# A two-layer transformer kernel: one-off setup work behind the first projections, three small jobs moved between engines, and later arrival times in the planner that writes the order

## The chip, the cores and the metric

One Trainium2 chip; the kernel runs on one of its cores. The metric is the device time of one execution in microseconds (us), median of several runs. Engines are named as in the profile: PE is TensorE (matmuls; PEld its weight loads), DVE is VectorE, ACT is ScalarE, POOL is GpSimd, SP is SyncE, which issues the DMAs.

## The reference

Two pre-norm transformer layers on x of shape (8, 1024, 256), 16 heads of 16 dimensions, all float32:

```
x = x + attention0(layernorm(x))      # causal softmax attention, 16 heads
x = x + ffn0(layernorm(x))            # gates from entmax over 16 experts
x = x + attention1(layernorm(x))      # low-rank q, k, v (folded to 256x256), rotary on half of each head
x = x + ffn1(layernorm(x))            # shared expert relu(x W1)^2 W2, and a router that adds nothing below a gate of 1
```

The part of `ffn0` that the change touches is entmax: 16 logits per token are normalised, sorted in descending order, and for every k the mean and the mean of squares of the k largest are needed, which are running sums over k divided by k:

```
mean   = cumsum(zs) / k
meansq = cumsum(zs * zs) / k
delta  = (1 - k * (meansq - mean**2)) / k
tau    = mean - sqrt(max(delta, 0))
```

The part of `attention1` is the rotary embedding, `x * cos + rot(x) * sin`.

## The kernel before, in words

**Tiles.** The 1024 tokens of a batch are two halves `c` of 512. Everything that is computed per half: a normalisation (`rstd` on POOL, `norm` on ACT, then `xt`, the transposed half, by PE and ACT), the q and k projection (`qk_`, `qk`) and the values (`v_`, `v`), the output projection (`yt`, `ao`), and the feed-forward pieces (`lg`, `logit`, `ent` 1 to 6, `at`, `g`, `h1`, `hid`, `z`, `fo` for layer 0; `rt`, `route`, `up`, `gate`, `down` for layer 1).

**Attention** works on units `u` of one batch, layer, half of the queries and four heads: 128 units. Float32 accuracy comes from three bfloat16 parts stacked along the contraction. A unit goes through these steps:
- `s`: scores with queries on partitions (L1092), read by DVE for the row maximum, one tile of up to 512 columns after another (`maximum`, L1688 on the tile with the causal diagonal, L1691 elsewhere).
- `mx`, `mt`: POOL splits the maxima in three parts, PE transposes them (L1105), DVE copies the 12 x 512 result to `mT` (`max_rows`, L1702), and SP writes it by DMA into the stacked queries `stk_q` (L947).
- `st`: the same scores transposed, maximum subtracted (L1116); ACT takes the exponential (L1428), POOL zeroes the part above the diagonal (L1595).
- `pv`: PE multiplies with the values (L1134); ACT copies (`o`), PE transposes back, DVE divides (`nm`).

PSUM: bank 5 collects `pv`; the other seven are handed out to whatever PE writes next, and PE waits until the last reader of a bank is done.

**q and k** are split for the stack by a chain over ACT and POOL (`rest`, `p1`, `p2`), for layer 1 behind the rotary embedding: POOL multiplies with cos (`rot`, L1571), DVE swaps neighbours (L1676) and multiplies with sin (L1678, `swap_pairs`), POOL adds (`add`, L1602), ACT rounds (`p0`). SP stores the parts in DRAM and loads each unit's stack from there (`ld`).

**Setup.** `fold` transposes and multiplies the low-rank weights of layer 1 into 256 x 256 ones and turns three feed-forward weights (PE L1253 to L1275, results copied by ACT L1463 and DVE L1864 in turn). It needs fifteen DMAs of weights, and DVE's memsets must be over.

**The order.** Nothing is scheduled by the chip: `program_order()` walks through a model of the engines while the kernel is built, and each engine executes its own instructions in the order of that one list, waiting on semaphores for the others. The model has a table `TIMES` (PE time, then engine and length of what follows), five chains of steps, seven banks, and a rank for each kind of step that could start now; `at` marks in a step's `("after", item)` what it must follow. `windows()` says which chains of steps run beside which attention passes: chain 0 must be finished in its window, chain 1 may go on longer. A step's start in the plan is the time when its inputs are ready by the model. If they come later on the chip, PE stands at that step, and everything behind it stands too.

In `program_order` the setup came as soon as the first window opened, as a fixed 18 us:

```
        if setup:
            plan.put(("setup",), plan.pe)
            plan.pe += 18.0
```

and `windows()` began with

```
    out = [([], [], loaded(0, 0) + loaded(0, 1) + projection(0, 0, 0)), ([(0, 0, 0)], [], projection(0, 0, 1))]
```

## Time and profile before

| | us |
|---|---|
| median of 3 runs | 3171.22 |
| lowest and highest run | 3166.03, 3175.09 |
| the profiled execution, its own time | 3174.84 |
| its span, first to last instruction | 3173.1 |
| busy: PE | 2888.2 (91%) |
| busy: DVE | 2165.5 (68%) |
| busy: ACT | 1905.3 (60%) |
| busy: POOL | 1138.1 (36%) |
| mean granted TensorE clock | 0.950 of 2.4 GHz |

The page of the profile has the busy time of each engine, the span in 40 slices with the granted clock, the chain of work that ended last, and the costliest groups of instructions. The trace behind it answers for any stretch: who waited for whom, the instructions in order of time, and busy times of chosen windows. In a row of the chain of waits or of groups, what stands behind `<-` is what the engine waited for.

### The profile page before, as it was taken

The page shows a single profiled execution, that of the slowest core. Times are in us where ns is not written, and L with a number is a line of the kernel's source. Part 1 is how long each engine was busy: PE and PEld are TensorE (multiplying, and loading weights), DVE is VectorE, ACT ScalarE, POOL GpSimd, SP SyncE. Part 2 cuts the span into 40 slices and gives each one's busy share as a digit, 9 for nine tenths or more (in the row PEclk, how much of TensorE's full clock was granted, in tenths as well). Part 3 has the DMA queues.
Part 4 walks back from the last instruction along what each step waited for, and adds up shares of the span by engine and source line. Part 5 has one row for each costly group of instructions (what it writes and reads, how often), then busy time and mean ns, then how long its engine had stood idle before and what let it go on. Part 6 is the DMA issues. An engine that isn't in the chain of part 4 may idle for free.

```text
span 3173.1 us, 55225 instructions
## 1 busy us (share of the span) xinstructions
PE 2888.2 (91%) x17687; PEld 1366.4 (43%) x17687; DVE 2165.5 (68%) x5957; ACT 1905.3 (60%) x3740; POOL 1138.1 (36%) x2476
## 2 busy tenths in 40 slices
PE   5787999999899998999989998999989999899996
PEld 3433443445344453445534454344534445344432
DVE  4573687765878558775577766776677865878582
ACT  3455655766466664767547674675746766466654
POOL 2314441435324342244513355132541435324421
PEclk9888999999899998999989999999989999899998
DMA  5602442323424253333514245132442324423230
GB/s 153 157 19 64 94 101 50 82 74 99 103 60 106 58 132 73 67 82 93 132 38 89 59 118 126 36 84 56 116 119 54 87 71 116 96 59 83 67 86 22
DMA packets 241196, 268.25 MB, mean 85 GB/s; under 512 B 19568, under 2 KB 208912, under 8 KB 240912
## 3 DMA queue, kind: packets, MB, share of 16 engines
q1 hardware_dynamic: 240912, 264.66, 35.5%
q8 instruction: 154, 2.52, 0.3%
q14 instruction: 130, 1.06, 0.1%
HBM read 162.35 MB, written 100.66 MB: 83 GB/s over the span
## 4 chain that ended last, share of the span: by engine, by line
PE 63%; DVE 18%; ACT 10%; issue 3%; DMA 3%; SPq 2%; POOL 1%; ACTq 0%; POOLq 0%; DVEq 0%
PE ps L1134 14%; PE ps L1116 13%; PE ps L1092 10%; PE ps L1072 6%; DVE mx L1691 6%; PE ps L1064 5%; ACT probs L1428 5%; DVE ps L1688 4%; PE ps L1210 4%; PE ps L1205 3%; PE ps L1197 2%; PE ps L1052 2%; DMA stk_k<-k 1%; ACT xn L1377 1%; PE ps L1097 1%
## 5 line engine op out<-in xcount | busy, mean ns | idle before, releaser
L1428 ACT ACTIVATE probs<-ps 128x512 f32<-128x512 f32 (+1 forms) x2432 | 1228.9, 595 | 429.0 <-PE ps L1116 421.6
L1691 DVE TENSOR_REDUCE mx<-ps 128x1 f32<-128x512 f32 (+2 forms) x1408 | 893.8, 683 | 238.8 <-PE ps L1092 132.6
L1092 PE MATMUL ps<-stk_k,stk_q 112*128 112x512 bf16 (+3 forms) x3072 | 809.9, 339 | 94.2 <-DVE mx L1691 31.2
L1595 POOL TENSOR_SCALAR_AFFINE_SELECT probs<-probs 128x128 f32<-128x128 f32 (+2 forms) x1408 | 479.9, 349 | 866.0 <-ACT probs L1428 836.5
L1116 PE MATMUL ps<-stk_q,stk_k 115*128 115x512 bf16 (+3 forms) x3072 | 758.3, 332 | 27.5 <-DMA stk_q<-mT 21.0
L1688 DVE CUSTOM_DVE_ANT_0 ps<-ps,mask_b 128x512 f32<-128x512 f32 (+1 forms) x1024 | 613.3, 649 | 137.7 <-PE ps L1092 133.2
L1134 PE MATMUL ps<-probs,vaug 128*17 128x512 f32 (+3 forms) x6144 | 586.9, 494 | 11.2 <-ACT probs L1428 6.7
L1092 PEld LDWEIGHTS ps<-stk_k,stk_q 112*128 112x128 bf16 x3072 | 276.4, 98 | 510.1 <-issue 363.5
L1116 PEld LDWEIGHTS ps<-stk_q,stk_k 115*128 115x128 bf16 x3072 | 269.0, 98 | 451.3 <-issue 206.2
L1064 PE MATMUL ps<-turned,wqkv 128*128 128x512 f32 x512 | 269.6, 615 | 9.9 <-ACT turned L1364 5.8
L1134 PEld LDWEIGHTS ps<-probs,vaug 128*17 128x17 f32 x6144 | 138.2, 97 | 313.3 <-issue 188.4
L1614 POOL CAST mparts<-mx 128x16 bf16<-128x16 f32 x128 | 26.4, 206 | 523.4 <-DVE mx L1696 309.3
L1377 ACT ACTIVATE xn<-x,shift,rstd 128x256 f32<-128x256 f32 x256 | 139.2, 618 | 90.8 <-POOL shift L1560 90.8
L1713 DVE RECIPROCAL rec<-ps 128x16 f32<-128x16 f32 x128 | 31.8, 248 | 219.2 <-PE ps L1142 218.7
L1580 POOL TENSOR_TENSOR scratch<-scratch,parts 128x512 f32<-128x512 f32 x128 | 148.2, 1158 | 81.1 <-ACT scratch L1395 43.3
L1449 ACT ACTIVATE scratch<-ps 128x512 f32<-128x512 f32 x128 | 75.5, 597 | 163.9 <-PE ps L1205 163.7
L1364 ACT ACTIVATE turned<-ps 128x512 f32<-128x512 f32 x192 | 114.3, 610 | 89.2 <-PE ps L1052 52.7
L1585 POOL TENSOR_TENSOR parts<-scratch,parts 128x512 bf16<-128x512 f32 x128 | 147.7, 1161 | 35.0 <-ACT parts L1407 34.9
L1721 DVE TENSOR_TENSOR x<-ps,x 128x512 f32<-128x512 f32 x128 | 88.1, 688 | 103.5 <-PE ps L1072 103.5
L1435 ACT ACTIVATE oT<-ps 128x512 f32<-128x512 f32 x128 | 77.9, 609 | 134.1 <-PE ps L1134 132.1
L1571 POOL TENSOR_TENSOR scratch<-scratch,cos 128x512 f32<-128x512 f32 x64 | 81.8, 1279 | 191.7 <-ACT scratch L1395 191.7
L1688 DVE DVE_READ_ACCUMULATOR2_ANT mx<- 128x1 f32 x1024 | 143.2, 140 | 0.0
(155 smaller groups left out, 3128.3 us busy)
## 6 DMA issues: line engine op xcount, KB each, us to landing
k<-parts SPq DMA_DIRECT2D x128, 384.0 KB, 3.5
stk_q<-q SPq DMA_DIRECT2D x256, 192.0 KB, 4.1
stk_k<-k SPq DMA_DIRECT2D x128, 384.0 KB, 6.7
q<-parts SPq DMA_DIRECT2D x64, 384.0 KB, 3.0
stk_k<-k SPq DMA_DIRECT2D x128, 192.0 KB, 4.2
x<-in_L_attn_x SPq DMA_DIRECT2D x16, 512.0 KB, 4.9
k<-parts SPq DMA_DIRECT2D x64, 128.0 KB, 3.5
stk_q<-q SPq DMA_DIRECT2D x128, 64.0 KB, 6.2
```

Source lines behind the costliest of these rows:

```text
L1064: ins = pe.matmul(pt, wqkv[l][:, kd, D * w + P * m:D * w + P * (m + 1)], xT(2 * l, b, c, kd), start=kd == 0, stop=kd == KD - 1)
L1072: ins = pe.matmul(pt[:, D * i:D * (i + 1)], left(kd)[:, cols], right(kd), start=kd == 0, stop=kd == n_k - 1)
L1092: ins = pe.matmul(out[:, width * a:width * (a + 1)], q, stk_k[0:ROWS_S, slot, h + a, BANK * p:BANK * p + width], start=a == 0, stop=a == n ...
L1116: ins = pe.matmul(out[:, width * k:width * (k + 1)], stk_k[0:ROWS, slot, h + k, P * j:P * (j + 1)], stk_q[0:ROWS, slot, h + k, cols], star ...
L1134: ins = pe.matmul(o_bank[32 * h:32 * h + DH + 1, cols], vaug[:, v, j % TPC, HG * g + h, :], probs[:, STEP[u, j] % PBUF, h, cols], start=j ...
L1377: ins = act.activation(xn[:, t, :], src[:, t, :], ACT.Identity, bias=shift[:, i, t:t + 1], scale=rstd[:, i, t:t + 1])
L1428: act.activation(probs[:, step % PBUF, h:h + k, cols], src, ACT.Exp, scale=SCALE)\
L1580: pool.tensor_tensor(q, q, parts[:, o % PRING, 0], ALU.subtract).then_inc(rest_ready, 1)
L1585: pool.tensor_tensor(parts[:, o % PRING, 2], qf[o % QRING], parts[:, o % PRING, 1], ALU.subtract)\
L1595: pool.affine_select(out=diag, in_=diag, compare_op=ALU.is_ge, fill=0.0, base=0, pattern=[[0, k]] * (k > 1) + [[1, P]], channel_multiplier ...
L1688: dve.tensor_tensor_reduce(tile, tile, mask_b[:, BANK - width:BANK], 1.0, LOWEST, ALU.add, ALU.max, most)\
L1691: dve.tensor_reduce(most, tile.rearrange("q (k w) -> q k w", k=k), AX.X, ALU.max)\
```

## The change

Seven things.
1. The setup becomes a step at the end of the first chain, behind the first projection, and the projection of the second half is put in chain 0 beside it. Transposed scores may not start before it. The normalisation and projection of the second batch's first half start one window earlier.
2. The running sums of entmax, eight instructions on DVE (two copies and two additions in part 3, two and two in part 4), become one `tensor_tensor_scan` over all 8 groups of 16: state = going * state + value, where `going` is 0 at each group's first element and 1 elsewhere. Two memsets fill `going` once.
3. The copy of the transposed maxima to `mT` goes from DVE to ACT.
4. The product with sin goes from DVE to POOL, into `rotate`, ahead of its addition. The swap stays on DVE.
5. The router's weights share a tile with entmax's projection; both narrow products now use all 24 columns, and the reader takes other columns. One memset goes.
6. Plan: `TIMES` of `rot` and `add` follow item 4; `max_rows` is planned on ACT with 0.6 us.
7. Plan: `LATER` adds 1.5 us to the time when a step that begins with `xt` may start, 0.7 us for `yt` and `at`; `ROWS_LATER` adds 1.5 us to the arrival of a unit's maxima in `stk_q`.

The `max_rows` in the diff stands in ACT's program; the one on DVE goes.

```diff
+SETUP_TIME, SETUP_LOADED = 20.0, 20.0
-    "rot": (0.0, ("DVE", 1.5), ("POOL", 1.0)), "add": (0.0, ("POOL", 1.2)), "p0": (0.0, ("ACT", 0.63)),
+    "rot": (0.0, ("DVE", 0.75), ("POOL", 1.25)), "add": (0.0, ("POOL", 2.6)), "p0": (0.0, ("ACT", 0.63)),
+LATER = {"xt": 1.5, "yt": 0.7, "at": 0.7}
+ROWS_LATER = 1.5
...
-    out = [([], [], loaded(0, 0) + loaded(0, 1) + projection(0, 0, 0)), ([(0, 0, 0)], [], projection(0, 0, 1))]
+    out = [([], projection(0, 0, 1), loaded(0, 0) + loaded(0, 1) + projection(0, 0, 0) + [([("setup",)], "")]),
+           ([(0, 0, 0)], [], loaded(1, 0) + projection(1, 0, 0))]
...
-            out.append(([(0, 0, 1)], attended(0, 0, 0) + first_ffn(0, 0), ahead + first))
+            out.append(([(0, 0, 1)], attended(0, 0, 0) + first_ffn(0, 0), first))
...
+        if step[0] and step[0][0][0] == "setup":
+            return max(time, SETUP_LOADED)
+        time += later(step)
...
-        end = self.on("DVE", self.pe + HOP, 0.4)
+        end = self.on("ACT", self.pe + HOP, 0.6)
...
-        self.rows[u] = self.transfer(end, 1.4, 0.1)
+        self.rows[u] = self.transfer(end, 1.4, 0.1) + ROWS_LATER
...
-        if u not in self.rows:
+        if u not in self.rows or ("setup",) not in self.at:
...
+            def max_rows(u):
+                pt = arrived(act, ("mt", u))
+                if MT["mt", u]:
+                    act.wait_ge(m_loaded, 16 * MT["mt", u])
+                act.activation(mT[:], pt[0:NP * HG, 0:BANK // 2].bitcast(BF16), ACT.Copy).then_inc(read_out(("mt", u)), 1)
...
             def rotate(*key):
+                pool.wait_ge(swap_ready, r + 1)
+                pool.tensor_tensor(qs[w], qs[w], sin[:, BANK * key[2]:BANK * (key[2] + 1)], ALU.mult).then_inc(sin_ready, 1)
                 pool.wait_ge(cos_ready, r + 1)
...
-                    a = cum[:, 0]
-                    for r, s in enumerate((1, 2)):
-                        z = cum[:, 1 + r % 2]
-                        dve.tensor_copy(z[:, :, 0:s], a[:, :, 0:s])
-                        link(dve.tensor_tensor(z[:, :, s:E0], a[:, :, s:E0], a[:, :, 0:E0 - s], ALU.add))
-                        a = z
+                    flat = [v.rearrange("p t k -> p (t k)") for v in (going[:], cum[:, 0], cum[:, 2])]
+                    link(dve.tensor_tensor_scan(flat[2], flat[0], flat[1], 0.0, ALU.mult, ALU.add))
```

Since the plan is walked anew, the order of all engines changes from the first instruction to the last. Three places show how.

**PE, the start of the program.** `ident,xn` is a half's `xt`, `turned,wqkv` and `wqkv,turned` its projections, `ident,probs` to `ident,scratch` the setup, `stk_k,stk_q` scores. Before:

```order
L1253 MATMUL ps<-ident,probs 128x128 x16
L1259 MATMUL ps<-probs,scratch 32x256 x8
L1266 MATMUL ps<-ident,x 128x128 x4
L1271 MATMUL ps<-ident,scratch 128x128 x8
L1275 MATMUL ps<-ident,scratch 128x128 x2
L1052 MATMUL ps<-ident,xn 128x128 x8
L1064 MATMUL ps<-turned,wqkv 128x512 x8
L1072 MATMUL ps<-wqkv,turned 128x256 x8
L1052 MATMUL ps<-ident,xn 128x128 x8
L1064 MATMUL ps<-turned,wqkv 128x512 x7
L1092 MATMUL ps<-stk_k,stk_q 128x512 x4
```

(of the first three rows each stands three times in turn.) With the change:

```order
L1058 MATMUL ps<-ident,xn 128x128 x8
L1070 MATMUL ps<-turned,wqkv 128x512 x8
L1078 MATMUL ps<-wqkv,turned 128x256 x8
L1058 MATMUL ps<-ident,xn 128x128 x8
L1070 MATMUL ps<-turned,wqkv 128x512 x8
L1078 MATMUL ps<-wqkv,turned 128x256 x8
L1259 MATMUL ps<-ident,probs 128x128 x16
```

Both halves are projected ahead of the setup, the second half first; the scores follow the setup.

**PE, behind the logits of batch 3, first half** (`ident,narrow`). `mparts` is `mt`, `stk_q,stk_k` is `st`, `probs,vaug` is `pv`. Before:

```order
L1177 MATMUL ps<-ident,narrow 128x128
L1092 MATMUL ps<-stk_k,stk_q 128x512 x2
L1092 MATMUL ps<-stk_k,stk_q 128x256 x2
L1097 MATMUL ps<-mask_b,ident_b 128x2x128
L1092 MATMUL ps<-stk_k,stk_q 128x256 x2
L1097 MATMUL ps<-mask_b,ident_b 128x2x128
L1092 MATMUL ps<-stk_k,stk_q 128x512 x4
L1092 MATMUL ps<-stk_k,stk_q 128x128 x4
L1097 MATMUL ps<-mask_b,ident_b 128x512
L1092 MATMUL ps<-stk_k,stk_q 128x512 x10
L1105 MATMUL ps<-ident_b,mparts 12x128 x4
L1092 MATMUL ps<-stk_k,stk_q 128x512 x2
```

With the change:

```order
L1183 MATMUL ps<-ident,narrow 128x128
L1098 MATMUL ps<-stk_k,stk_q 128x512
L1140 MATMUL ps<-probs,vaug 17x128 x4
L1098 MATMUL ps<-stk_k,stk_q 128x512 x2
L1148 MATMUL ps<-ident,oT 128x128 x4
L1122 MATMUL ps<-stk_q,stk_k 128x512 x4
L1098 MATMUL ps<-stk_k,stk_q 128x512
L1122 MATMUL ps<-stk_q,stk_k 128x512
L1098 MATMUL ps<-stk_k,stk_q 128x384
L1122 MATMUL ps<-stk_q,stk_k 128x512
L1098 MATMUL ps<-stk_k,stk_q 128x384
L1140 MATMUL ps<-probs,vaug 17x512 x4
```

Before, PE's program has nothing but scores there, nearly two units of them; now it has transposed scores and `pv` between them.

**POOL, a rotary piece of a later batch.** `scratch,cos` is `rot`, `scratch<-scratch` the addition, `probs` the causal zeroes. Before:

```order
L1571 TENSOR_TENSOR scratch<-scratch,cos 128x512
L1585 TENSOR_TENSOR parts<-scratch,parts 128x512
L1602 TENSOR_TENSOR scratch<-scratch 128x512
L1580 TENSOR_TENSOR scratch<-scratch,parts 128x512
L1585 TENSOR_TENSOR parts<-scratch,parts 128x512
L1595 AFFINE_SELECT probs<-probs 128x128 x8
```

With the change:

```order
L1585 TENSOR_TENSOR scratch<-scratch,cos 128x512
L1609 AFFINE_SELECT probs<-probs 128x128
L1609 AFFINE_SELECT probs<-probs 128x2x128 x2
L1609 AFFINE_SELECT probs<-probs 128x4x128
L1594 TENSOR_TENSOR scratch<-scratch,parts 128x512
L1615 TENSOR_TENSOR scratch<-scratch,sin 128x512
L1618 TENSOR_TENSOR scratch<-scratch 128x512
L1599 TENSOR_TENSOR parts<-scratch,parts 128x512
```

The product with sin stands directly ahead of the addition, and both ahead of whatever the planner puts behind them.

## Rows read from the trace of the kernel before

**Rows 1.** The page: busy times, and the granted clock in 40 slices.
```profile
PE 2888.2 (91%) x17687; PEld 1366.4 (43%) x17687; DVE 2165.5 (68%) x5957; ACT 1905.3 (60%) x3740; POOL 1138.1 (36%) x2476
...
PEclk9888999999899998999989999999989999899998
```
**Rows 2.** Who waited for whom, PE over the span: us in total, times, longest.
```profile
PE ps L1052 <- ACT xn L1377: 40.8, 18, 8.2
PE ps L1092 <- DVE mx L1691: 31.2, 52, 1.8
PE ps L1183 <- DVE cum L1802: 23.6, 7, 3.6
PE ps L1116 <- DMA stk_q<-mT: 21.0, 14, 2.7
...
PE ps L1134 <- ACT probs L1428: 6.7, 12, 1.5
...
PE ps L1134 <- POOL probs L1595: 3.6, 12, 0.8
```
**Rows 3.** Busy time by window: six stretches of 36 us, two short ones, one for comparison.
```profile
core 0: us, PE busy (x) PEld busy (x) DVE busy (x) ACT busy (x) POOL busy (x), PEclk, DMA share, GB/s
823.00:859.00 36.00, 26.55 (x103) 7.15 (x99) 34.22 (x109) 11.30 (x22) 11.09 (x13) 0.67 0.19 63
1198.00:1234.00 36.00, 26.51 (x102) 8.74 (x102) 34.90 (x109) 10.97 (x22) 12.35 (x14) 0.67 0.27 81
...
2717.00:2753.00 36.00, 26.40 (x103) 8.74 (x102) 34.90 (x111) 11.14 (x22) 12.36 (x14) 0.67 0.29 84
305.00:335.00 30.00, 21.06 (x81) 9.37 (x80) 23.50 (x88) 11.54 (x24) 9.92 (x23) 0.74 0.40 106
...
1280.00:1400.00 120.00, 118.18 (x813) 53.94 (x805) 96.35 (x254) 88.73 (x180) 46.41 (x96) 1.00 0.38 86
```
**Rows 4.** Timeline of DVE inside the second of these stretches.
```profile
1210.42 5.47 DVE L1691 TENSOR_REDUCE mx<-ps 128x2 f32<-128x512 f32 x9
...
1224.18 0.41 DVE L1702 COPY mT<-ps 12x512 bf16<-12x512 bf16 x1
```
**Rows 5.** Timeline of the start, PE, DVE and POOL: start, length, what, idle before it.
```profile
19.34 1.41 DVE L1655 BATCH_NORM_STATS2 st<-x 128x6 f32<-128x256 f32 x4
...
20.03 3.65 PE L1253 MATMUL ps<-ident,probs 128*128 128x128 f32 x16 [20.03 <-DMA scratch<-in_L_attn_Wv_up]
...
40.94 1.94 PE L1052 MATMUL ps<-ident,xn 128*128 128x128 f32 x8 [2.53 <-ACT xn L1377]
43.65 9.15 PE L1064 MATMUL ps<-turned,wqkv 128*128 128x512 f32 x16 [0.78 <-ACT turned L1364]
52.64 3.62 PE L1072 MATMUL ps<-wqkv,turned 128*128 128x256 f32 x16
...
72.87 0.70 DVE L1688 CUSTOM_DVE_ANT_0 ps<-ps,mask_b 128x512 f32<-128x512 f32 x1 [31.95 <-PE ps L1092]
...
88.11 3.60 PE L1092 MATMUL ps<-stk_k,stk_q 112*128 112x512 bf16 x10 [4.75 <-DMA stk_k<-k]
...
101.45 1.97 PE L1052 MATMUL ps<-ident,xn 128*128 128x128 f32 x8 [8.21 <-ACT xn L1377]
...
105.99 1.49 PE L1116 MATMUL ps<-stk_q,stk_k 115*128 115x512 bf16 x3
```
**Rows 6.** Groups of instructions by shape: count, busy us, mean ns, idle before.
```profile
L1702 DVE COPY mT<-ps 12x512 bf16<-12x512 bf16 x128 | 52.3, 408 | 98.6 <-PE ps L1105 97.9
L1678 DVE TENSOR_TENSOR scratch<-scratch,sin 128x512 f32<-128x512 f32 x64 | 51.7, 808 | 2.2
L1364 ACT ACTIVATE turned<-ps 128x512 f32<-128x512 f32 x192 | 114.3, 610 | 89.2 <-PE ps L1052 52.7 <-PE ps L1149 36.0
L1571 POOL TENSOR_TENSOR scratch<-scratch,cos 128x512 f32<-128x512 f32 x64 | 81.8, 1279 | 191.7 <-ACT scratch L1395 191.7
```
**Rows 7.** One line's instructions: ns min/median/max.
```profile
L1678 DVE TENSOR_TENSOR scratch<-scratch,sin x64: 691/693/1599, 269.2 to 3004.1; 128x512 f32<-128x512 f32 x64
```

More of the change, by code:

```diff
@@ L162, in loaded @@
     return before + [([("load", b, c)], ""), ([("stat", b, c)], "")]
+SETUP_TIME, SETUP_LOADED = 20.0, 20.0
 TIMES = {
     "most": (0.0, ("DVE", 0.19)), "mx": (0.0, ("POOL", 1.15)),
-    "load": (0.0, ("SP", 6.0)), "stat": (0.0, ("DVE", 2.2)), "rstd": (0.0, ("POOL", 1.35)), "norm": (0.0, ("ACT", 0.8)),
+    "setup": (SETUP_TIME,), "load": (0.0, ("SP", 6.0)), "stat": (0.0, ("DVE", 2.2)), "rstd": (0.0, ("POOL", 1.35)), "norm": (0.0, ("ACT", 0.8)),
     "xt": (0.44, ("ACT", 0.6)), "yt": (0.44, ("ACT", 0.6)), "qk_": (0.86,), "qk": (0.86, ("ACT", 0.9)),
-    "rot": (0.0, ("DVE", 1.5), ("POOL", 1.0)), "add": (0.0, ("POOL", 1.2)), "p0": (0.0, ("ACT", 0.63)),
+    "rot": (0.0, ("DVE", 0.75), ("POOL", 1.25)), "add": (0.0, ("POOL", 2.6)), "p0": (0.0, ("ACT", 0.63)),
     "rest": (0.0, ("POOL", 1.16)), "p1": (0.0, ("ACT", 0.63)), "p2": (0.0, ("POOL", 1.16)),
@@ L310, in give @@
                     self.open[n] = b
+            if item[0] == "setup":
+                self.busy["ACT"] = self.busy["DVE"] = self.pe
+                self.free = [min(end, self.pe) for end in self.free]
             for engine, length in rest:
@@ L471, in normalise, with later @@
         self.put(("nm", u), end)
+def later(step):
+    item = step[0][0] if step[0] else ("",)
+    return 0.0 if item[0] in ("xt", "yt") and item[-1] else LATER.get(item[0], 0.0)
 def takes_time(step):
@@ L499, in program_order @@
     line = 0.0
-    setup = False
     def size(chain):
@@ L526, in program_order @@
             sizes, given = [size(chain) for chain in plan.chains[:2]], [0.0, 0.0]
-            if units and units[0] == 0:
-                setup = True
         moved = True
@@ L537, in program_order @@
                     moved = True
-        if setup:
-            plan.put(("setup",), plan.pe)
-            plan.pe += 18.0
-            plan.free = [min(time, plan.pe) for time in plan.free]
-            for engine in ("ACT", "DVE"):
-                plan.busy[engine] = plan.pe
-            setup = False
         plan.load_stack()
@@ L757, in transformer_kernel @@
         wout2T = sb("wout2T", [R, D])
-        wr = sb("wr", [P, KD, STRIP])
         ws1 = sb("ws1", [P, KD, FE])
@@ L775, in transformer_kernel @@
         gate = sb("gate", [P, B, TT, NE])
+        going = sb("going", [P, 2 * TPC, E0])
         gmax = sb("gmax", [P, NC * B])
@@ L983, in _ @@
                 (wo[1][:], wc_d.rearrange("(k p) n -> p k n", p=P)),
-                (wr[:, :, 0:NE], wr_d.rearrange("(k p) n -> p k n", p=P)),
+                (projw[:, :, E0:E0 + NE], wr_d.rearrange("(k p) n -> p k n", p=P)),
                 (ws1[:], ws1_d.rearrange("(k p) f -> p k f", p=P)),
@@ L1323, in _ @@
                 elif kind == "rt":
-                    narrow_product(item, 3, *key, wr)
+                    narrow_product(item, 3, *key, projw)
                 elif kind == "route":
@@ L1494, in _ @@
                     exponentials(*key)
+                elif kind == "mt":
+                    max_rows(*key)
                 elif kind == "o":
@@ L1676, in swap_pairs @@
                 dve.stream_shuffle(qs[w], qf[o % QRING], [i ^ 1 for i in range(32)]).then_inc(swap_ready, 1)
-                dve.wait_ge(swap_ready, r + 1)
-                dve.tensor_tensor(qs[w], qs[w], sin[:, BANK * key[2]:BANK * (key[2] + 1)], ALU.mult).then_inc(sin_ready, 1)
             def maximum(u, i, h, p):
@@ L1766, in entmax @@
                     link(dve.tensor_tensor(zq, zs, zs, ALU.mult))
-                    a = cum[:, 0]
-                    for r, s in enumerate((1, 2)):
-                        z = cum[:, 1 + r % 2]
-                        dve.tensor_copy(z[:, :, 0:s], a[:, :, 0:s])
-                        link(dve.tensor_tensor(z[:, :, s:E0], a[:, :, s:E0], a[:, :, 0:E0 - s], ALU.add))
-                        a = z
-                elif part == 4:
-                    a = cum[:, 2]
-                    for r, s in enumerate((4, 8)):
-                        z = cum[:, 1 + r % 2]
-                        dve.tensor_copy(z[:, :, 0:s], a[:, :, 0:s])
-                        link(dve.tensor_tensor(z[:, :, s:E0], a[:, :, s:E0], a[:, :, 0:E0 - s], ALU.add))
-                        a = z
+                    flat = [v.rearrange("p t k -> p (t k)") for v in (going[:], cum[:, 0], cum[:, 2])]
+                    link(dve.tensor_tensor_scan(flat[2], flat[0], flat[1], 0.0, ALU.mult, ALU.add))
+                elif part == 4:
                     inv = kidx[:, 1, :].rearrange("p (a k) -> p a k", a=1).broadcast_to([P, 2 * TPC, E0])
-                    link(dve.tensor_tensor(cum[:, 1], a, inv, ALU.mult))
+                    link(dve.tensor_tensor(cum[:, 1], cum[:, 2], inv, ALU.mult))
                     link(dve.tensor_tensor(zt[:], mean, mean, ALU.mult))
@@ L1810, in router @@
                 b, c = item[1:]
-                pt = arrived(dve, item)[:, 0:P].rearrange("p (t e) -> p t e", t=TPC)[:, :, 0:NE]
+                pt = arrived(dve, item)[:, 0:P].rearrange("p (t e) -> p t e", t=TPC)[:, :, E0:E0 + NE]
                 dve.tensor_copy(zc[:, :, 0:NE], pt).then_inc(read_out(item), 1)
@@ L1873, in fold @@
                 copy(wout2T[:], D)
-            for w in (projw, wr):
-                dve.memset(w[:], 0.0)
+            dve.memset(projw[:], 0.0)
             dve.memset(up, 0.0).then_inc(up_zeroed, 1)
+            dve.memset(going[:, :, 1:E0], 1.0)
+            dve.memset(going[:, :, 0:1], 0.0)
             dve.memset(vaug[:], 1.0)
@@ L1898, in _ @@
                     greater(*key)
-                elif kind == "mt":
-                    max_rows(*key)
                 elif kind == "nm":
```

5 lines of the change are left out of this document (removed).

## The prediction

> **What bounds the kernel now.** I read the page first. PE is busy for 91% of the span and no other engine comes near [rows 1], so time can only be won where PE stands still or runs at the lower level of its clock. The clock line shows that this happens in places, not everywhere: eights stand among the nines from start to end [rows 1]. The list of waits says for what PE stands: for `xt` 40.8 us, for VectorE's row maxima 31.2, for entmax's result 23.6 in seven waits of up to 3.6, for the maxima's DMA 21.0 [rows 2].
>
> The windows say where. In six stretches of 36 us, about 380 us apart, of which three are shown, VectorE is busy 34 to 35 of 36 us, PE finishes about 103 matmuls, and the granted clock is 0.67 [rows 3]: PE has fallen to the 1.2 GHz level while it starves. In an undisturbed stretch PE makes 813 matmuls in 120 us, 6.8 per us, at clock 1.00 [rows 3]. So 102 matmuls are worth 15 us, and each stretch loses 21. VectorE is the bound there, and any microsecond of it removed or moved away counts in full; elsewhere it hides. The cause is in the order: behind the logits PE's program holds scores alone, a 512-column tile takes PE 0.21 us at 2.4 GHz and VectorE 5.47/9 = 0.61 us [rows 4], and entmax and the copies to `mT`, 0.41 each [rows 4], share VectorE with them.
>
> **The change, part by part.** I cost the new order by counting. For every piece of 15 us of PE work I add what VectorE must do beside it, with the mean durations of the trace, and call what exceeds the 15 us the excess. For the order before this gives 21.1 in six places, where the windows lost 21. I trust the count for that reason.
>
> *1. VectorE's crowded stretches.* With the change the same count gives 6.6 at most in those six batches: transposed scores and `pv` now stand between the scores. That is 6 x 14.5 = 87 us. In the four other crowded places (rows 3 show one, 305 to 335 us) the counts are 16.3, 11.5, 10.2 and 10.0 before and 15.4, 8.2, 9.5 and 18.2 now; the last, near the end, gets worse. Their sum rises by 3.3. **Term: -84.** Part of it is the work that leaves VectorE: 52.3 us of `mT` copies and 51.7 of sine products [rows 6], and eight short running-sum instructions per entmax (about 1.4 us) for one scan. The scan has no row. It is no shorter than a 128-element product, 0.29, and I allow it twice that; 16 of them make 5 or 9 us over the kernel, either way hidden but for the crowded places. I take it inside the count at 0.35.
>
> *2. The start.* Before, the setup began at 20.03, when its last DMA landed, and the first scores reached VectorE at 72.87 [rows 5]. Now: statistics of both halves, 19.34 + 2 x 2.0 = 23.4; `rstd` 1.2 and the first `norm` 2.2 put the first `xt` at 26.9. From an `xt` to the end of that half's values took 56.3 - 40.9 = 15.3 at the lower clock [rows 5], so 42.2. The second half waits for its `rstd` behind five POOL instructions, until about 44.3, and needs 13.2 at the full clock: 57.5. The setup took 18.4; it gains 1.8, since its first sixteen transposes need no cold 3.65 us [rows 5]. It ends at 74.1, and scores start there, 1.6 later than before. But before, 33 us passed from the first score to the first transposed score at 105.99, with two waits of 4.75 and 8.21: for a unit's stack, and for x of batch 1, whose load stood late in SP's queue behind stores [rows 5]. Now that load is issued right behind the first unit's stack, ahead of all fifteen weights. What is left is VectorE's work: two units at 6.5 us (eleven tiles at 0.5 to 0.65), three tiles of the third and one set of statistics, 17 us. The first transposed score comes at about 91.5, 14.5 earlier; but the third unit's other scores, 4 us of VectorE, were behind it then and are still to come. **Term: -10.5**; at worst nothing, if the loads come late, at best -18.
>
> *3. Later arrivals.* Between a unit's `mt` and its first `st` the order before had under 2.5 us of PE work 12 times in 128, now 4 times; between logits and `at` of a first half VectorE's excess falls from 8.1 to 5.9; ahead of the two first `xt` of layer 0's feed-forward PE has 8.9 and 1.7 us of work instead of 1.8 and none. Of the waits in [rows 2] that could save 8 of 21.0, 13 of 23.6 and 8 of 40.8. These places partly lie in the crowded stretches, so I take half. **Term: -15**, bounds 0 and -29. What was late is then next: the stack loads, with no change made to them.
>
> *4. `mT` on ScalarE.* No row has a 12 x 512 read by ScalarE. The nearest is its copy of 128 x 512, 610 ns [rows 6]; below, VectorE's 408. 128 x 0.61 is 78 us on an engine busy at 60%, queued among exponentials, with all transposed scores of the unit behind it by way of SP and the DMA. PE's waits for exponentials at `pv` are 6.7 us in all [rows 2], so ScalarE has room, and the plan's extra 1.5 us cover the delay. **Term: +10**, bounds 0 (hidden) and +78 (all on the path).
>
> *5. Sine on GpSimd.* A product there takes 1.28 us [rows 6]; 64 make 82 us on an engine busy at 36%. Queued behind it are the causal zeroes, for which PE waited just 3.6 us in all [rows 2], and the split chain whose parts SP stores. **Term: +6**, bounds 0 and +82.
>
> Here VectorE and GpSimd touch: the sine product is 693 ns at its median, 808 in the mean and 1599 at most [rows 6, 7], because it overlaps with the cosine product. The move takes 64 x 0.115 = 7 us of such delay away from VectorE (within term 1).
>
> *6. The router's tile, one memset less, two small ones more:* nothing. The memsets run in the first 19 us, beside loads until 20.03 [rows 5].
>
> Sum: -84 - 10.5 - 15 + 10 + 6 = **-93.5 us**. The profiled execution took 3174.84, so 3081.3; the median of the runs is 3.6 below it: **3078**.
>
> **The rivals.**
> - *The crowding moves instead of going* (0.18). The planner's own durations for entmax are unchanged, and VectorE's total falls only 5%. If half of the 84 comes back in other places: 3120. For it: the last place, which my count shows worse. Against: the count before met all six.
> - *More goes than counted* (0.10): PE stays at the upper clock, and all 29 us of term 3 are won; with a further 14 from stretches of 0.67 turning to 1.00: 3050.
> - *GpSimd's reads block VectorE's small operations* (0.08). The 1599 ns product waited some 0.9 us, most of a 1.28 us GpSimd operation [rows 6, 7]. The new sine products are such operations, and entmax is a chain of about thirty dependent ones with two operands in SBUF. One hit of 1.28 in each of 16 chains gives 20 us: 3098. The Trainium skill ("SBUF — State Buffer", Who interferes with whom) says that a VectorE instruction with two SBUF inputs and a GpSimd one that reads SBUF block each other for the whole instruction. By that rule, the trace's 1599 ns fits.
> - *GpSimd becomes the wait, and the kernel slower* (0.06). Sine and addition stand in one block of 2.55 us ahead of the causal zeroes, 64 times. If a `pv` or a stack load waits for the whole block each time, that is +163 instead of +6: 3234. It decides from (93.5 + 6)/64 = 1.55 us per block upward. Against: GpSimd's idle time and four buffers of probabilities.
> - *Nothing comes of the new order* (0.06): terms 1 and 3 fail, and the start pays for 4 and 5. 3171 to 3177.
>
> **How the numbers follow.** My forecast has 0.52: 3078, between 3060 and 3100 with the bounds of terms 2 and 3 and a fifth of term 1. The range 3045 to 3135 takes in the first three rivals and leaves the other two and the tails out. What a measurement of this kernel can tell from no change is about 0.3%, 9.5 us. Faster: 0.52 + 0.18 + 0.10 + 0.08 = 0.88; the same 0.06; slower 0.06.
>
> **What would show it.** Right: no stretch of 36 us with only a hundred matmuls, the granted clock line without its eights in mid-span and a mean above 0.95, first transposed score near 92 us, waits for `mx` and for `mT`'s DMA down by a third or more. Wrong in term 1: VectorE busy over 95% for 30 us somewhere per batch. Wrong in 4 or 5: PE's waits for ACT's exponentials or POOL's zeroes [rows 2] grown past 20 us, or many waits for stack loads. The forecast is wrong as a whole if the time lies above 3120 with the six stretches gone.

## The result, and the profile after

| | before | changed kernel |
|---|---|---|
| median, us | 3172.29 (3166.03 to 3175.09) | 3038.59 (3037.22 to 3042.73) |
| span of the profiled execution | 3173.1 | 3035.5 |
| mean granted clock | 0.950 | 0.974 |

The ratio is 0.9583 (95% interval 0.9566 to 0.9601): the change gains 133.7 us (4.2%). I had forecast 3078 and a range from 3045 to 3135; the sign was right, the gain was larger than the range allowed by 6 us.

The page of the changed kernel, the rows that answer to [rows 1]:

```profile
PE 2824.8 (93%) x17687; PEld 1352.6 (45%) x17687; DVE 2068.7 (68%) x5654; ACT 1959.6 (65%) x3868; POOL 1216.7 (40%) x2540
...
PEclk9898999999999999999999999999999999999988
```

PE's idle time fell from 284.9 to 210.7 us (span minus busy), by 74; its busy time fell by 63 for the same 17687 matmuls. The eights have gone from the middle of the clock line.

Who waited for whom, PE over the span (compare [rows 2]):

```profile
PE ps L1058 <- ACT xn L1383: 55.4, 8, 27.2
PE ps L1098 <- DVE mx L1705: 13.7, 52, 1.6
PE ps L1148 <- ACT oT L1447: 11.6, 24, 0.9
PE ps L1111 <- POOL mparts L1633: 11.2, 8, 4.3
PE ps L1140 <- POOL probs L1609: 10.2, 17, 1.0
...
PE ps L1189 <- DVE cum L1801: 7.2, 8, 1.4
...
PE ps L1098 <- DMA stk_k<-k: 6.6, 11, 1.2
PE ps L1098 <- DVE mx L1702: 6.0, 18, 1.5
...
PE ps L1122 <- DMA stk_q<-mT: 2.2, 3, 1.0
```

The first row holds one wait of 27.2 us, PE's very first, which stands where before a wait of 20 for the setup's last DMA stood [rows 5]; without it 28.2 are left of 40.8. Waits for VectorE's maxima at L1705 fell from 31.2 to 13.7, for entmax from 23.6 to 7.2, for the maxima's DMA from 21.0 to 2.2.

Busy time by window, the changed kernel, same columns as [rows 3]: three stretches of 36 us that hold the logits' places of three batches, one near the end, and a quiet one.

```profile
846.00:882.00 36.00, 32.91 (x186) 12.60 (x185) 29.72 (x73) 19.59 (x41) 8.29 (x27) 0.91 0.20 40
1204.00:1240.00 36.00, 32.90 (x188) 12.65 (x187) 29.69 (x73) 19.81 (x42) 7.91 (x26) 0.91 0.20 40
2638.00:2674.00 36.00, 32.63 (x183) 12.74 (x183) 29.46 (x74) 19.61 (x40) 8.51 (x28) 0.91 0.20 40
...
1280.00:1400.00 120.00, 115.81 (x708) 56.47 (x708) 81.59 (x237) 86.91 (x173) 59.54 (x107) 1.00 0.40 101
2888.00:2924.00 36.00, 29.17 (x100) 11.43 (x100) 31.73 (x80) 3.73 (x8) 0.85 (x4) 0.69 0.60 131
```

Where PE made 102 matmuls at a mean clock of 0.67 it now makes 183 to 188 at 0.91. The six stretches lie 358 us apart ((2638 - 846)/5) where they lay 379 apart ((2717 - 823)/5). So most of the gain is a shorter batch, 20 us each. The last row is the place near the end that my count had shown worse: 100 matmuls in 36 us, at 0.69.

To see where the gain arises I put both kernels' score tiles side by side by how much PE work lies ahead of them. The changed kernel leads by 10 us at 140 us of PE work, 14 at 240, 29 at 540, 53 at 640, 44 at 740, 66 at 1040, 94 at 1440, 118 at 1840, 161 at 2240, 156 at 2440. It jumps at the crowded stretches, gives part of a jump back, and gains between them. Behind 2440 lies the place near the end: the lead there falls from 156 to the 138 of the whole spans, so this one place costs 18 us, where my count had 8.2. One wait of PE for a normalisation, 10.4 us, is part of it.

### The profile page after: what moved, and what is told of

Its sections match the earlier page's. It is cut to its first block, busy times and chain, and to the rows that moved or that the text cites. A ratio compares the mean times of both kernels' runs of the same rounds, so it can differ in the third digit from the quotient of the medians.

```text
span 3035.5 us, 55103 instructions
## 1 busy us (share of the span) xinstructions
PE 2824.8 (93%) x17687; PEld 1352.6 (45%) x17687; DVE 2068.7 (68%) x5654; ACT 1959.6 (65%) x3868; POOL 1216.7 (40%) x2540
## 4 chain that ended last, share of the span: by engine, by line
PE 69%; DVE 16%; ACT 7%; issue 3%; DMA 2%; POOL 1%; SPq 1%; DVEq 0%; ACTq 0%; POOLq 0%
PE ps L1140 16%; PE ps L1122 13%; PE ps L1098 12%; PE ps L1078 6%; PE ps L1070 6%; DVE mx L1705 5%; PE ps L1216 4%; ACT probs L1434 4%; DVE ps L1702 3%; PE ps L1211 3%; DMA stk_k<-k 2%; PE ps L1058 2%; PE ps L1203 2%; ACT xn L1383 1%; PE ps L1103 1%
## 5 line engine op out<-in xcount | busy, mean ns | idle before, releaser
L1705 DVE TENSOR_REDUCE mx<-ps 128x1 f32<-128x512 f32 (+2 forms) x1408 | 887.0, 682 | 239.9 <-PE ps L1098 177.2
L1702 DVE CUSTOM_DVE_ANT_0 ps<-ps,mask_b 128x512 f32<-128x512 f32 (+1 forms) x1024 | 614.2, 649 | 322.4 <-PE ps L1098 319.9
L1098 PE MATMUL ps<-stk_k,stk_q 112*128 112x512 bf16 (+3 forms) x3072 | 773.4, 333 | 35.9 <-DVE mx L1705 13.7
L1122 PE MATMUL ps<-stk_q,stk_k 115*128 115x512 bf16 (+3 forms) x3072 | 754.2, 329 | 18.3 <-ACT probs L1434 9.0
L1140 PE MATMUL ps<-probs,vaug 128*17 128x512 f32 (+3 forms) x6144 | 581.4, 490 | 15.5 <-POOL probs L1609 10.2
L1070 PE MATMUL ps<-turned,wqkv 128*128 128x512 f32 x512 | 263.4, 609 | 6.7 <-ACT turned L1370 3.6
L1594 POOL TENSOR_TENSOR scratch<-scratch,parts 128x512 f32<-128x512 f32 x128 | 148.3, 1160 | 55.8 <-ACT scratch L1401 28.2
L1441 ACT ACTIVATE mT<-ps 12x512 bf16<-12x512 bf16 x128 | 74.2, 580 | 122.3 <-PE ps L1111 122.2
L1702 DVE DVE_READ_ACCUMULATOR2_ANT mx<- 128x1 f32 x1024 | 143.5, 140 | 0.0
L1216 PE MATMUL ps<-scratch,win 128*128 128x512 f32 x256 | 132.5, 600 | 11.5 <-ACT scratch L1461 11.5
L1078 PE MATMUL ps<-wo,turned 128*128 128x256 f32 x512 | 133.5, 389 | 6.7 <-ACT turned L1370 6.7
```

Source lines behind the costliest of these rows:

```text
L1070: ins = pe.matmul(pt, wqkv[l][:, kd, D * w + P * m:D * w + P * (m + 1)], xT(2 * l, b, c, kd), start=kd == 0, stop=kd == KD - 1)
L1078: ins = pe.matmul(pt[:, D * i:D * (i + 1)], left(kd)[:, cols], right(kd), start=kd == 0, stop=kd == n_k - 1)
L1098: ins = pe.matmul(out[:, width * a:width * (a + 1)], q, stk_k[0:ROWS_S, slot, h + a, BANK * p:BANK * p + width], start=a == 0, stop=a == n ...
L1122: ins = pe.matmul(out[:, width * k:width * (k + 1)], stk_k[0:ROWS, slot, h + k, P * j:P * (j + 1)], stk_q[0:ROWS, slot, h + k, cols], star ...
L1140: ins = pe.matmul(o_bank[32 * h:32 * h + DH + 1, cols], vaug[:, v, j % TPC, HG * g + h, :], probs[:, STEP[u, j] % PBUF, h, cols], start=j ...
L1216: pe.matmul(acc, win2[:, k, :], hsb[k % 3], start=k == 0, stop=k == OC - 1)\
```

## The experiments

Each was timed beside the kernel before on the same chip; the medians of the kernel before lay between 3168.5 and 3173.1. "Order" is the list that all engines follow; "work" is what the instructions of each step are (maxima copied by ACT, sine on POOL, one scan). In the diffs, lines that begin with `# e` say in words what a run changes.

### Work and order apart

```diff
# e1: items 2 to 5 of the change; program_order, TIMES, windows as before
# e2: program_order, TIMES, windows, LATER of the change; instructions as before
```

> The order of the kernel before with the changed instructions: mT copied by ScalarE, sine product on GpSimd, running sums by one scan, shared router tile. The change gained 134 us. Theory 1, the order is what counts (the crowded stretches of VectorE are a matter of order; counted excess in the six is 18.4 against 21.1 before): about 3150, 15 to 30 us below the kernel before, six stretches at a granted clock below 0.75 still there. Theory 2, the work taken off VectorE is what counts wherever it is the bound: 3110 or lower. If it is slower than 3172, ScalarE and GpSimd take back what VectorE gives.

> The changed order with the instructions of the kernel before: mT copied by VectorE, sine product on VectorE, eight instructions for the running sums. Theory 1 (order): most of the gain is there, 3060 to 3085; the counted excess of VectorE over PE is 259 us against 306 before and 198 with the change. Theory 2 (work): above 3110. Together with the run of the new instructions in the old order it tells whether the two parts add up to 134 us.

Measured: the work alone 3154.11 us, ratio 0.9935 (0.9919 to 0.9952), 19 less; the order alone 3113.16, ratio 0.9812 (0.9794 to 0.983), 60 less. Together they give 134, not 79: in the old order the new work is worth 19, in the new order 75. The work pays in the order that was planned for it. e1 came out as its first theory said; e2 missed the 3060 to 3085 of its first theory and lies just inside the second's "above 3110".

### Later arrivals: removed, and alone

```diff
# e3, in the changed kernel
-LATER = {"xt": 1.5, "yt": 0.7, "at": 0.7}
-ROWS_LATER = 1.5
+LATER = {}
+ROWS_LATER = 0.0
# e4: the kernel before with LATER and ROWS_LATER as in the change, nothing else
```

> The change without its later arrivals in the plan (LATER empty, ROWS_LATER 0); all else as changed, so the order is planned anew. Theory A, the later arrivals break up the crowded stretches and take the waits for xt, at and mT: 3110 or higher, waits of PE for mT's DMA back at some 20 us. Theory B, the six crowded stretches go with the other changes of the plan (setup, windows, VectorE's shorter items; the count of excess here is 212 against 198) and the later arrivals are worth only the waits, 15 to 30 us: 3055 to 3068.

> The kernel before with nothing but the later arrivals in its plan. Theory A: 3090 to 3110, since these alone make the order. Theory B: 3120 to 3150; the count of VectorE's excess is 288 against 306, with the six crowded stretches at 11 instead of 21, and the waits for mT and at go.

Measured: without them 3103.9 us, ratio 0.9778 (0.9762 to 0.9794); alone on the kernel before 3140.24, ratio 0.9895 (0.9878 to 0.9911). 3103.9 lies between what the two theories gave, 3140.24 is as the second said. Later arrivals seem to be worth 65 us, where my third term said 15 and at most 29. PE's waits in e3:

```profile
PE ps L1058 <- ACT xn L1383: 71.4, 17, 27.2
PE ps L1122 <- DMA stk_q<-mT: 23.8, 27, 2.0
PE ps L1098 <- DVE mx L1705: 18.1, 35, 2.3
```

The waits for which the term was made come back, 16 us at `xt` and 22 at the maxima's DMA: 38 of the 65. The rest stays unexplained by them. The crowded stretches don't come back: in a worst place of e3, the 36 us from 1136, PE makes 160 matmuls at a clock of 0.91.

### The three jobs put back, one at a time, order unchanged

```diff
# e5: in the changed kernel, max_rows on DVE again
-act.activation(mT[:], pt[0:NP * HG, 0:BANK // 2].bitcast(BF16), ACT.Copy)
+dve.tensor_copy(mT[:], pt[0:NP * HG, 0:BANK // 2].bitcast(BF16))
# e6: the product with sin on DVE again, behind the swap
# e7: eight running-sum instructions instead of the scan
```

> The change in its own order, with the copy of the maxima back on VectorE (nothing else differs, the order is the same item for item). All the moved work together is worth 74.6 us in this order (3113.2 against 3038.6). If VectorE's length counts evenly, the 128 copies of 0.41 us are 52.3 of some 131 us taken off it, so 0.4 of 74.6: 3068. If what counts is that the copy waits in VectorE's queue behind row maxima while PE and the DMA wait for it (12.6 us of PE waits for mT and 12.1 for its DMA in the run with the old work), it is worth 45 or more: above 3080.

> The change in its own order, with the sine product back on VectorE. Even share by length (51.7 of 131 us): 3068. Theory of small gain: rotary work stands where VectorE has room, GpSimd's blocks of 2.5 us cost some of it back: 3045 to 3055. If GpSimd's move costs more than it gives, below 3038.

> The change in its own order, with the eight instructions of the running sums instead of the scan. By length, some 22 us of VectorE less the scans: 3050. If the entmax chain's end is waited for by PE (at), each of 16 chains is 1.4 us longer: 3055 to 3060. If it is hidden: 3040.

Measured: e5 3085.76 (ratio 0.9739, 0.9719 to 0.9759), e6 3056.86 (0.9642, 0.9624 to 0.966), e7 3051.61 (0.9625, 0.9607 to 0.9643). Against the changed kernel the copy to `mT` is worth 47 us, the sine product 18, the scan 13; the sum, 78.5, meets the 75 of all three together. These four kernels have one order, so nothing but the work differs. But that order was planned with the copy and the sine product where they now are; an order planned anew with one of them put back was not run, and might lose less. e6 lies between two of its theories, e7 at the first. The copies, in the changed kernel and in e5 (groups by shape):

```profile
L1441 ACT ACTIVATE mT<-ps 12x512 bf16<-12x512 bf16 x128 | 74.2, 580 | 122.3 <-PE ps L1111 122.2
```
```profile
L1708 DVE COPY mT<-ps 12x512 bf16<-12x512 bf16 x128 | 52.3, 409 | 146.0 <-PE ps L1111 145.8
```

By the profiles, VectorE's busy time grows by 41 us in e5 (2110.0 against 2068.7), 48 in e6 (2116.4), 19 in e7 (2087.5). So a microsecond of VectorE's busy time cost 1.1 us of the kernel for the copy, 0.4 for the sine product and 0.7 for the sums.

e5 lies above 3080, where a wait in VectorE's queue had put it. The copy is slower on ScalarE by 171 ns, and the kernel is faster by 47 us. On VectorE it stands among row maxima, and its unit's transposed scores wait for it by way of SP. The traces have the delay: from the end of a unit's transposes to the start of its copy 0.89 us pass in the mean in e5 (at most 4.9; over half a microsecond for 47 of 128), 0.30 in the changed kernel (at most 3.1; 17 of 128). So the copy is done 0.42 us earlier on the slower engine. PE's waits in e5 show what hangs on it; in the changed kernel the first two are 6.6 and 2.2, and the third is none:

```profile
PE ps L1098 <- DMA stk_k<-k: 17.2, 19, 1.5
PE ps L1122 <- DMA stk_q<-mT: 12.5, 11, 1.7
...
PE ps L1098 <- DVE mT L1708: 10.8, 10, 3.0
```

### The start

```diff
# e8: the changed kernel with the setup first again (18.0 as before) and the first windows of before
# e12: the changed kernel, order unchanged
             dve.memset(vaug[:], 1.0)
+            first = [item[1:] for item in ORDER if item[0] == "stat"][:2]
+            for b, c in first:
+                dve.wait_ge(x_loaded[x_slot(b, c)], 16)
+                statistics(0, c, x[:, x_slot(b, c)], range(TPC))
             for i in range(NBUF):
                 dve.memset(stk_k[ROWS_A:P, i, :, :], -1.0)
...
             def load_stack(u):
+                if u == 0:
+                    sp.wait_ge(ready0, 2)
```

> The change with the setup and the first windows of the kernel before; the rest of the plan is walked anew, so later pieces may shift. My term for the start was 10.5 us: 3049. The traces show the changed kernel 10 us ahead after the first 140 us of PE work, so 3046 to 3052 if the start alone differs; if the new windows also help later, 3060.

> The changed kernel, same order, with VectorE's statistics of the first two halves ahead of its memsets of the stacked keys, 10.4 us of them; the first stack load waits for the memsets. The first xt of PE, which waits 27.2 us, comes at about 16. Theory A (with one order, what is won at the start is kept to the end, since every engine's work only shifts): 11 us less, 3024 to 3030. Theory B (the start is given back at the next load, or at the setup, whose weights land at 20 and whose copies wait for other things): 3035 to 3040.

Measured: with the old start 3035.38, ratio 0.9575 (0.9557 to 0.9592), the same as the changed kernel. That is no second draw of the order: from item 412 of 8514 on, e8's list is the changed kernel's, item for item. It is faster than each of its expectations (3046 to 3060), so the new start and the new first windows bring nothing that lasts. With the first statistics early 3025.44, ratio 0.9541 (0.9517 to 0.9564). The start of e12, DVE and PE:

```profile
5.71 1.34 DVE L1673 BATCH_NORM_STATS2 st<-x 128x6 f32<-128x256 f32 x4
...
11.37 3.47 DVE L1886 MEMSET stk_k<- 32x4096 bf16 x1 [0.91 <-issue]
```
```profile
14.16 1.94 PE L1060 MATMUL ps<-ident,xn 128*128 128x128 f32 x8 [14.16 <-ACT xn L1385]
```

In the changed kernel the same statistics begin at 19.41, behind the memsets, though x had landed (e12 waits for its second half only, until 8.36), and PE begins at 27.21. By the medians this kernel beats the changed one by 13 us and is the fastest of the study, as the first theory said (3024 to 3030). Of the 13 us of PE's earlier start, the two profiled executions have 12 left at 240 us of PE work and 9 at the end; they are the slowest of e12's four runs and the fastest of the changed kernel's. So with the order kept most of an earlier start stays, perhaps all.

### Nearby orders

The order came out of planned durations and arrivals. I moved one or two of them by 0.02 to 0.1 us; e11 leaves out one group of later arrivals.

```diff
# e9: xt and ROWS_LATER 1.6   # e10: xt 1.6, ROWS_LATER 1.4   # e11: LATER = {}, ROWS_LATER 1.5
# e13: before, "mx" 1.25 for 1.15      # e14: before, "v" 0.65 for 0.6
# e15: changed, "mx" 1.17 for 1.15     # e16: changed, "fo" 1.92 for 1.90
# e17: e3 with "mx" 1.17               # e18: e3 with "xt" 0.65 for 0.6
```

> The changed kernel with the two largest later arrivals raised by a tenth of a microsecond: xt and maxima's rows 1.6 us instead of 1.5. Theory A (later arrivals give slack: steps stand behind enough other work, and that is what the 65 us are): a tenth more slack changes nothing that can be measured, 3038 within 10, so 3028 to 3048. Theory B (the order is a walk in which any small change moves everything behind it, and the number 1.5 found a good one): the count of VectorE's excess over pieces of 15 us of PE work is 245 us for this order instead of 198, and the time comes out 25 to 50 us higher, 3064 to 3090.

> The changed kernel with xt 1.6 and maxima's rows 1.4 us. Theory A (slack): 3028 to 3048. Theory B (the order decides through VectorE's excess): the count is 192 us, 6 below the changed kernel's, so 3028 to 3048 as well. The run tells whether orders with a low count are good in general: a time above 3060 would say that the count misses what matters.

> The changed kernel with later arrivals of the maxima's rows alone (1.5 us), none for xt, yt and at. Slack theory: the waits for the maxima's DMA go, those for xt and for entmax come back (71 instead of 55 us and 10 more): 3055 to 3065. Theory of the order: the count is 227 us, between 198 (3039) and 212 to 259 (3104 and above): 3065 to 3090.

> The kernel before with one planned duration changed: the splitting of the maxima 1.25 us instead of 1.15, instructions as before. Its order leaves that of before at item 115 of 8514; in six places the count of VectorE's excess is 12 instead of 21, its sum 315 instead of 306. Theory of the draw (small changes redraw the order, here too): the time differs from 3171 by 15 us or more, either way; with 12 instead of 21 in six places I expect the lower side, 3120 to 3155. Theory of slack (small changes do nothing): 3161 to 3181.

> The kernel before with the planned copy of the values 0.65 us instead of 0.6. The count has twelves instead of the six 21s, sum 303 instead of 306. Theory of the draw: off 3171 by 15 us or more, 3110 to 3155. Theory of slack: 3161 to 3181.

> The changed kernel with the planned splitting of the maxima 1.17 us instead of 1.15. Its order leaves at item 106; count 216 instead of 198. Theory of the draw with a lucky number: 3060 to 3105, as its neighbours. Theory of slack: 3028 to 3048.

> The changed kernel with one planned duration, VectorE's part behind the feed-forward output, 1.92 us instead of 1.90. The order is the same up to item 1323 of 8514; count 238 instead of 198. Theory of the draw with a lucky number: 3060 to 3105, and up to PE's work of that item no difference to the changed kernel. Theory of slack: 3028 to 3048.

> The changed kernel without later arrivals and with the planned splitting of the maxima 1.17 us instead of 1.15, the partner of the order that gave 3076 with them. Theory A (later arrivals are worth the 15 us of my third term once the draw is taken out): orders without them lie about 15 to 25 us above those with them, 3086 on average, so 3090 to 3120, and the mean of the three without them 3098 to 3112. Theory B (nothing but the draw): this and the next scatter around 3086, at least one of them below 3085.

> The changed kernel without later arrivals and with the planned copy of a transposed half 0.65 us instead of 0.6. Theory A: 3090 to 3120. Theory B: this and the run before scatter around 3086, at least one of them below 3085.

| kernel | us, median | ratio (interval) | count of VectorE's excess |
|---|---|---|---|
| before | 3171 | | 306 |
| e13 before, `mx` 1.25 | 3214.77 | 1.0139 (1.0122 to 1.0156) | 315 |
| e14 before, `v` 0.65 | 3187.54 | 1.0049 (1.0033 to 1.0066) | 303 |
| changed kernel | 3038.59 | 0.9583 (0.9566 to 0.9601) | 198 |
| e15 changed, `mx` 1.17 | 3075.63 | 0.9701 (0.9685 to 0.9718) | 216 |
| e16 changed, `fo` 1.92 | 3081.22 | 0.9702 (0.9678 to 0.9726) | 238 |
| e10 changed, 1.6 and 1.4 | 3085.05 | 0.9729 (0.9698 to 0.976) | 192 |
| e9 changed, 1.6 and 1.6 | 3102.16 | 0.9777 (0.975 to 0.9803) | 245 |
| e17 no later arrivals, `mx` 1.17 | 3086.39 | 0.9733 (0.9715 to 0.975) | not on record |
| e3 no later arrivals | 3103.9 | 0.9778 (0.9762 to 0.9794) | 212 |
| e11 rows' alone | 3106.57 | 0.9794 (0.9768 to 0.982) | 227 |
| e18 no later arrivals, `xt` 0.65 | 3134.24 | 0.9887 (0.9868 to 0.9907) | not on record |

The theory of slack fell at once: a tenth of a microsecond more gives back 64 us. Of four orders next to the changed kernel's the best is 37 us slower; their mean is 3086. The two next to the order before are slower than it by 16 and 43, though my count had made me expect both faster (3120 to 3155 and 3110 to 3155). Where later arrivals are left out, three orders have a mean of 3108; with them, the four neighbours have 3086. The difference of 22 us is about my term of 15, but the orders scatter by 11 and 24 us (standard deviation) around these means, so that it is not settled by seven draws. Neither theory of e17 and e18 held as written: the mean of three is the first's, but 3086.39 and 3134.24 lie on both sides of its 3090 to 3120, and none is below the 3085 of the second. e11 and e9 came out slower than both of their theories.

e14 is the sharpest test of my first term. Its stretches, by window (columns as before):

```profile
872.00:908.00 36.00, 31.32 (x195) 10.77 (x194) 30.87 (x100) 19.31 (x40) 10.22 (x31) 0.86 0.22 40
1254.00:1290.00 36.00, 31.27 (x195) 10.76 (x193) 31.16 (x101) 19.58 (x40) 10.16 (x31) 0.86 0.21 40
```

and its waits:

```profile
PE ps L1052 <- ACT xn L1377: 52.9, 34, 8.1
...
PE ps L1149 <- DVE y L1716: 13.3, 9, 1.7
```

The stretches with a hundred matmuls have gone in it too: each loses 12.4 us instead of 21, some 50 us less over the six. Yet the kernel is 15 us slower. At 540 us of PE work it lies 2.6 behind the kernel before, at 640, past a stretch, 8.5 ahead, at 740 again 1.5 behind: what was won is lost within 100 us, in many small waits, at `xt` 34 instead of 18, at `y` 13.3 us. My count shows no gain either, if it is summed over all pieces and not over the largest ones: 303 against 306. e13 is like it (12.8 in two places of each batch, sum 315), with more of the same waits:

```profile
PE ps L1052 <- ACT xn L1377: 56.0, 28, 8.3
PE ps L1116 <- DMA stk_q<-mT: 39.5, 21, 5.2
...
PE ps L1092 <- DVE y L1716: 21.3, 13, 2.9
PE ps L1116 <- ACT probs L1428: 20.7, 23, 1.7
```

## Why the prediction was right or wrong

**What bounds the kernel, and the sign: right.** PE waits, VectorE's crowded stretches, and most of the gain by way of both.

**The step that failed** is the sum itself: it took one planned order to be worth what my count of VectorE's excess said, with no term and no width for the order as such, and it entered the copy and the sine product as costs of 10 and 6. Orders planned from nearly the same durations run 37 to 64 us slower than this one, and with the order held the two moves gain 47 and 18.

**Term 1, -84: its local numbers were close, its sum was not the gain.** I counted 6.6 for the six stretches; they lose 8.4 to 8.7, measured over 15 us of PE work. That is 6 x 12.4 = 74 won instead of 87. Five other places (16.1, 14.2, 12.1, 11.2 and 9.4 before, 12.8, 15.2, 9.7, 10.9 and 18.0 now) lose 3.6 more in all, where I had counted 3.3 more. These place by place losses are my own reckoning from both traces; no row shown has them, and the five depend on where a piece of 15 us is begun. So about 71 us of the 134 lie in the places that I added up, and 63 elsewhere; the last of these places costs 18 if its surroundings are taken in, which leaves about 60 and 74. And e14 shows that places cleared in this way need not make a kernel faster. The weak step was "for the order before this gives 21.1 in six places, where the windows lost 21. I trust the count for that reason": it had met one order, in its largest places. Summed over all pieces it sorts the family of before (303 to 315) from that of the change (192 to 245), but inside the latter it is no guide: 192 gave 3085, 198 gave 3039, 245 gave 3102, 212 gave 3104.

**Terms 4 and 5, +10 and +6: wrong in sign.** I priced the copy to `mT` and the sine product as loads on their new engines, and what VectorE is freed of as part of term 1 alone, without a number. For the whole order the count does have one: 259 with the old work, 198 with the new, 61 for a measured 75. In the changed kernel's order the copy is worth 47 us, the sine product 18. Taking the copy off VectorE brought nine tenths of its whole duration (52.3 us), and more than VectorE's busy time fell (41): it left a queue of row maxima on which PE's banks and the unit's DMA both hang. "Elsewhere it hides" was false for it. The scan brought 13 us. What e1 adds: in the old order all three together bring 19. The gains of 47 and 18 hold for the new order alone. I had no way to see from one order what they bring in another.

**Term 2, -10.5: nothing.** The first transposed score came at 97.45, not 91.5; I had left out PE's 4.3 us wait for POOL's parts of the first maxima and 1.5 for the next `xt`. With the old start and the rest of the change it comes at 96.90 (e8). So the lead of 10 us at 140 us of PE work is not the new start's: e8 is 3 us further ahead there, and is as fast at the end. The kernel before with nothing but later arrivals (e4), and so with the old start, leads by about 14 us at the same place.

**Term 3, -15: as a slack about right, as a number wrong.** Removing the later arrivals costs 65 us; the spread of orders around is as large as that. With neighbours averaged their worth is 22, not settled.

**The cause of the miss.** My four other terms made -78.5, and the change without later arrivals measured -69. Neighbours of the changed kernel have a mean of 3086, 8 above my 3078. Both agreements are in part luck: term 2 brought nothing, terms 4 and 5 had the wrong sign, and single orders scatter by 11 to 24 us. The 47 us between them and 3039 I call the draw: what the one order that came out at 1.5 us has over those around it. I gave no term and no width to this, though the range needed some 20 us on each side for it. The two neighbours of before say that it, too, is on the good side. I didn't test what in the changed kernel's order makes it better than its neighbours; the traces show only where: PE is idle for 211 us instead of 227 to 236 in e9, e10, e15 and e16, and its busy time is 20 to 42 us lower for the same matmuls. Two waits are longer in all four: for the row maxima at L1702 14.5 to 18.3 us instead of 6.0, and for a unit's stack (`stk_k<-k`) 11 to 29 instead of 6.6. Why this order avoids them stays open.

**The rivals and the signs.** The crowding that moves instead of going (3120) is what e14 does, but not what the changed kernel does. GpSimd as the wait did not come: PE's waits for its zeroes grew from 3.6 to 10.2 us, for the split maxima from 3.8 to 11.2. Its reads do block VectorE, but hardly more than before; the last section has the rows. My reading of [rows 7] was wrong as well: of the 17 sine products over 0.85 us two began beside the cosine product, one beside the addition, and 14 beside the split's subtractions (L1580, L1585), the one of 1599 ns among them. "More goes than counted" (3050, chance 0.10) was nearest, and one of its reasons held: the clock rose in the stretches (0.67 to 0.91, between the two levels). Of the signs that I had named for being right, the mean clock and the shorter waits came; the first transposed score came at 97.45 instead of near 92, and one stretch with a hundred matmuls is left near the end.

## What to carry to other kernels

Where a planner writes the order for an in-order machine, one order is one draw: move a planned duration by a few hundredths of a microsecond, time three or four neighbours of both kernels, and only then say what a change is worth; and keep the good draw, since it is free. Price a move off a crowded engine in the order that will run, with one job put back at a time: same order, different work leaves no draw in between, though it favours the work that the order was planned for. A small copy ahead of a DMA and a long wait belongs where it starts soonest, here 0.30 instead of 0.89 us after its input, even if it takes longer there. Look at the first wait of the first engine: memsets ahead of data that has landed were worth 13 us.

## What the runs showed of the hardware

A scan of 128 elements takes 0.42 us, and three times that beside a GpSimd product of 512 columns. The scan's durations (ns min/median/max) in the changed kernel:

```profile
L1777 DVE TENSOR_TENSOR_SCAN cum<-going,cum x16: 423/424/1334, 192.0 to 2781.2; 128x128 f32<-128x128 f32 x16
```

and one of the long ones, VectorE and GpSimd in order of time (start, length):

```profile
1348.95 0.23 DVE L1774 TENSOR_TENSOR cum<-cum 128x64 f32<-128x64 f32 x1
1349.21 1.33 DVE L1777 TENSOR_TENSOR_SCAN cum<-going,cum 128x128 f32<-128x128 f32 x1
1350.57 0.29 DVE L1780 TENSOR_TENSOR cum<-cum,kidx 128x128 f32<-128x128 f32 x1
```
```profile
1349.10 1.16 POOL L1594 TENSOR_TENSOR scratch<-scratch,parts 128x512 f32<-128x512 f32 x1 [0.50 <-ACT scratch L1401]
```

The scan began 0.11 us behind the GpSimd product and ended 0.28 us behind its end, so two thirds of a lone scan's time came after it. Alone it takes 424 ns; five of sixteen took 1.33 us, 4.5 us over the kernel, each of them begun beside the product of L1594. I had allowed 0.29 to 0.58, without this. The Trainium skill ("SBUF — State Buffer", Who interferes with whom) says that a VectorE instruction with two SBUF inputs contends with a GpSimd instruction that reads SBUF, and that the shared ports are locked by one of the two at a time. This row agrees, 0.90 us over. Another scan, at 302.44, lay wholly beside a GpSimd power of four columns (1.01 us) and took 424 ns: there the trace shows no delay.

The other instructions of the chain are hit too, as this one is:

```profile
L1800 DVE SCALAR_TENSOR_TENSOR cum<-zc x16: 224/226/1082, 204.9 to 2791.3; 128x64 f32<-128x64 f32 x16
```

Over all sixteen entmax chains VectorE loses 24 us in 32 such hits (what each took over its line's median, where that is above 0.15 us), about the 20 us of my rival. But in the kernel before it lost 17 in 34 hits, and all 32 stand beside the split's subtractions or the causal zeroes, none beside the sine product. So the move of the sine brought none of it.

A read of 12 x 512 by ScalarE from PSUM took 580 ns where VectorE takes 409: few partitions are hardly cheaper there than 128 (613 ns for 128 x 512 in the changed kernel).
